# Cross attention: row sums from ScalarE's accumulator, taken off the row maxima as a logarithm

## The reference

```python
qp = q @ Wq.T
k, v = jnp.split(latent_kv @ Wkv_expand.T, 2, axis=-1)      # 16 heads of 32
scores = jnp.einsum('bhqd,bhkd->bhqk', qh, kh) / jnp.sqrt(32)
scores = jnp.where(causal, scores, finfo.min)               # 256 x 256 for each batch and head
attn = jax.nn.softmax(scores, axis=-1)
out = jnp.einsum('bhqk,bhkd->bhqd', attn, vh)
return out.reshape(b, sq, 512) @ Wout.T
```

## Time and profile before

| | |
|---|---|
| times of three runs | 1062.95 (median), 1061.24, 1067.86 us |
| profiled execution | 1065.82 us, span 1064.1 us |
| mean granted clock of PE over the span | 0.977 |
| busy: PE, DVE, ACT, POOL | 1005.4, 669.4, 454.0, 261.4 us |
| cross attention | from 293.9 us to 550.8 us of the span |

### The profile page before, as it was taken

How to read it: one execution, slowest core, us unless ns; L and a number is a source line. 1 busy time by engine, 2 the same in 40 slices (tenths; PEclk the granted TensorE clock), 3 DMA queues, 4 the chain that set the end, 5 groups by cost and what they waited for, 6 DMA issues and landing times. The chain is left out here.

```text
span 1064.1 us, 18069 instructions
## 1 busy us (share of the span) xinstructions
PE 1005.4 (94%) x6352; PEld 857.4 (81%) x6352; DVE 669.4 (63%) x1515; ACT 454.0 (43%) x803; POOL 261.4 (25%) x362
## 2 busy tenths in 40 slices
PE   7899999999979999999979989999999999999996
PEld 5688888888868888887757778989988999778785
DVE  4837546378266677776566837777777775253576
ACT  5523414236125455454534216666665664221210
POOL 4610010103143333333412012312231220503040
PEclk9999999999987999999998989999999999899999
DMA  4503013022786788877622247788778783615042
GB/s 162 194 1 119 0 59 148 0 79 97 210 224 148 218 204 233 232 218 200 212 104 73 82 144 251 246 268 279 236 263 276 253 258 110 221 36 178 19 158 79
DMA packets 87248, 172.79 MB, mean 162 GB/s; under 512 B 8113, under 2 KB 36017, under 8 KB 85393
## 3 DMA queue, kind: packets, MB, share of 16 engines
q1 hardware_dynamic: 81072, 150.21, 45.2%
q0 software_dynamic: 6112, 21.76, 6.2%
HBM read 131.05 MB, written 37.49 MB: 158 GB/s over the span
## 5 line engine op out<-in xcount | busy, mean ns | idle before, releaser
L45 PE MATMUL a_ps_proj<-region_a_rounded,arena 128*128 128x512 f32 x272 | 107.8, 396 | 10.7 <-DVE region_a_rounded L369 6.2
L45 PE MATMUL e_ps_h<-e_x_lo,e_gu_hi 128*128 128x256 f32 (+1 forms) x384 | 110.5, 288 | 3.8 <-DVE e_x_lo L2189 1.3
L962 DVE CUSTOM_DVE_ANT_0 b_dump<-b_ps_s,b_mask 128x128 f32<-128x128 f32 (+1 forms) x256 | 80.3, 353 | 48.5 <-PE b_ps_s L1157 45.3
L46 PE MATMUL e_ps_h<-e_x_hi,e_gu_lo 128*128 128x256 f32 (+1 forms) x384 | 107.5, 280 | 0.0
L47 PE MATMUL e_ps_h<-e_x_hi,e_gu_hi 128*128 128x256 f32 (+1 forms) x384 | 107.4, 280 | 0.0
L46 PE MATMUL a_ps_proj<-region_a_rounded,arena 128*128 128x512 f32 x272 | 106.7, 392 | 0.0
L47 PE MATMUL a_ps_proj<-region_a_rounded,arena 128*128 128x512 f32 x272 | 106.6, 392 | 0.0
L388 DVE SCALAR_TENSOR_TENSOR f_region_b<-a_ps_proj,a_taps,f_region_b 128x510 f32<-128x510 f32 (+2 forms) x96 | 71.7, 746 | 41.0 <-ACT f_region_b L328 38.7
L2195 DVE TENSOR_TENSOR e_gu_lo<-f_region_a,e_gu_hi 128x704 fp32r<-128x704 f32 x92 | 81.2, 886 | 16.6 <-ACT e_gu_hi L2101 16.1
L848 ACT ACTIVATE b_pt<-b_ps_x 128x384 f32<-128x384 f32 x128 | 61.8, 487 | 60.0 <-PE b_ps_x L1181 59.8
L762 POOL TENSOR_SCALAR_AFFINE_SELECT b_pt<-b_pt 128x256 f32<-128x256 f32 x128 | 54.3, 428 | 123.0 <-ACT b_pt L848 122.5
(11 more groups left out here) (418 smaller groups left out, 2665.5 us busy)
## 6 DMA issues: line engine op xcount, KB each, us to landing
f_region_a<-we_gate_up SPq DMA_DIRECT2D x88, 352.0 KB, 5.2
qk_split<-arena SPq DMA_DIRECT2D x24, 512.0 KB, 5.4
y_slots<-f_region_b SPq DMA_DIRECT2D x16, 512.0 KB, 3.7
f_x_next<-x SPq DMA_DIRECT2D x6, 1024.0 KB, 7.4
b_sk<-qk_split SPq DMA_DIRECT2D x24, 256.0 KB, 4.1
b_sq<-qk_split SPq DMA_DIRECT2D x24, 256.0 KB, 5.7
f_region_a<-we_down SPq DMA_DIRECT2D x12, 512.0 KB, 4.4
f_region_b<-we_down SPq DMA_DIRECT2D x11, 512.0 KB, 4.1
```

Of the source, the lines that this page charges most:

```text
L45: pe.matmul(out, a_hi, b_lo, start=first, stop=False)
L46: pe.matmul(out, a_lo, b_hi, start=False, stop=False)
L962: ins = dve.tensor_tensor_reduce(dump[:, n % 2, cols], ps_s[:, n % 2, cols], mask[:, cols], -1.0, 3e38, ALU.add, ALU.min, peak[:, u, k, i: ...
```

## The change

The sums of the exponentials are no longer made by PE. As before, DVE's maxima leave the masked scores, negated (now also multiplied by the scale of the scores), in `dump`; ACT now takes the exponential of each head's `dump`, with the row's maximum as bias, and its accumulator gives the row sum (`totals`, two instructions for each head, on 128 and 256 columns). When eight heads are done, ACT takes the logarithm (`logs`), DVE takes it off the negated maxima (`shifts`), and that, in place of the maxima, is transposed and loaded below the queries. The second exponentials are then normalised already. `pick`, `invert`, `keep`, `spread_out` and `normalize` go.

To make room on ACT, DVE rounds x, queries and values from PSUM by a copy, and also waits for that copy before it subtracts; ACT rounds `ps_o` straight into `a_hi`, DVE makes `a_lo`. The two DMAs of `load_peaks` move from SP to POOL. `peaks` stands in step 3 of both halves, `shifts` in step 1. DVE's maxima wait for the totals of two heads before (`dump` has two buffers).

```diff
@@ gpsimd
+            def load_peaks(b, u):
+                pool.wait_ge(m_lo_done, half_count(b, u))
+                for r, m in ((K_ROWS, m_hi), (K_ROWS + 1, m_lo)):
+                    pool.dma_start(sq[b % 2][r:r + 1, u].bitcast(F32), m[:, u].bitcast(F32)).then_inc(m_loaded, 16)
...
-                        if t and u == 0 and i in (3, 4):
-                            rest(t - 1, i - 3)
+                        if u == 0 and i == 4:
+                            load_peaks(t, 1)
+                        if u == 1 and i == 4 and real(t + 1):
+                            load_peaks(t + 1, 0)
@@ scalar
-            act.preload_act_table_set("exp_and_others")
+            act.preload_act_table_set("natural_log_exp_and_others")
...
+            def totals(b, u, i):
+                n = order(b, u, i)
+                act.wait_ge(max_done, n + 1)
+                for k, cols in ((0, slice(0, P)), (1, slice(P, 3 * P))):
+                    ins = act.activation(dump[:, n % 2, cols], dump[:, n % 2, cols], ACT.Exp, scale=-1.0,
+                                         bias=peak[:, u, k, i:i + 1], accum_out=total[:, u, k, i:i + 1])
+                ins.then_inc(total_done, 1)
+
+            def logs(b, u):
+                act.wait_ge(total_done, order(b, u, UH - 1) + 1)
+                if b:
+                    act.wait_ge(shift_done, half_count(b - 1, u))
+                act.activation(log_total[:, u], total[:, u], ACT.Ln).then_inc(log_done, 1)
...
                         exponent(t, u, i)
+                        if i == 0 and (u == 0 or real(t + 1)):
+                            totals(t + u, 1 - u, UH - 1)
+                            logs(t + u, 1 - u)
+                        if i and real(t + 1):
+                            totals(t + 1, u, i - 1)
                         fill(t, u, i)
...
-                keep(t)
-            for u in range(2):
-                attended(B - 1, u)
+                for u in range(2):
+                    attended(t, u)
@@ vector
             def turned(b, u):
-                dve.wait_ge(xkq_hi_done, x_count(b, u))
+                dve.wait_ge(xkq_ready, x_count(b, u))
...
+                dve.tensor_copy(hi, ps_pj[:, u]).then_inc(xq_hi_done, 1)
+                dve.wait_ge(xq_hi_done, x_hi_count(b, u))
+                dve.tensor_tensor(lo, ps_pj[:, u], hi.bitcast(F32), ALU.subtract).then_inc(xkq_lo_done, 1)
...
+            def shifts(b, u):
+                dve.wait_ge(log_done, half_count(b, u))
+                if b:
+                    dve.wait_ge(m_ready, half_count(b - 1, u))
+                dve.tensor_tensor(shift[:, u], peak[:, u], log_total[:, u], ALU.subtract).then_inc(shift_done, 1)
...
                 if n >= 2:
-                    dve.wait_ge(max_done, n - 1)
+                    dve.wait_ge(total_done, n - 1)
...
-                        if t >= 1 and u == 0 and i in (1, 2):
-                            normalize(t - 1, i - 1)
-                        if u == 0 and i == 5:
+                        if t >= 1 and u == 0 and i < 2:
+                            attended(t - 1, i)
+                        if u == 0 and i == 1:
+                            shifts(t, 1)
+                        if u == 0 and i == 4:
                             peaks(t, 1)
-                        if u == 1 and i == 2 and real(t + 1):
+                        if u == 1 and i == 1 and real(t + 1):
+                            shifts(t + 1, 0)
+                        if u == 1 and i == 4 and real(t + 1):
                             peaks(t + 1, 0)
@@ tensor
             def peaks(b, u):
-                pe.wait_ge(max_done, order(b, u, UH - 1) + 1)
+                pe.wait_ge(shift_done, half_count(b, u))
...
             def attend(b):
-                pe.wait_ge(exp_done, HEADS * (b + 1) - 1)
-                for c in range(DC):
-                    pe.wait_ge(cut_done, HEADS * b + HC * (c + 1))
-                    for r in range(BT):
-                        for h in range(HC):
-                            mm = pe.matmul(ps_x[h * HD:(h + 1) * HD, 0, r * P:S], pick[:, c],
-                                           pt[:, HC * c + h, 2 * r * P:(2 + r) * P],
-                                           start=c == 0 and r == 0, stop=c == DC - 1 and r == BT - 1)
-                mm.then_inc(sums_o_ready, 1)
...
-                        if t >= 1 and u == 0 and i == 1:
-                            spread_out(t - 1)
-                        if u == 0 and i == 4:
+                        if u == 0 and i == 3:
                             peaks(t, 1)
```

More of the change, by code:

```diff
@@ L551, in cross_attention @@
         peak = sb("peak", [P, 2, BT, UH])
+        total = sb("total", [P, 2, BT, UH])
+        log_total = sb("log_total", [P, 2, BT, UH])
+        shift = sb("shift", [P, 2, BT, UH])
         m_split = sb("m_split", [HD + UH, 2, S], F32R)
@@ L777, in _ @@
             pool.memset(bln.power[:], -0.5).then_inc(consts, 1)
[L778 to L785, removed]
+            pool.wait_ge(consts, 5)
             for k in sk:
                 pool.memset(k[K_ROWS:M_ROWS].bitcast(F32), 1.0).then_inc(consts, 1)
-            pool.wait_ge(consts, 14)
+            pool.wait_ge(consts, 7)
+            load_peaks(0, 0)
             for t in range(0, B):
@@ L866, in fill @@
                             keys(b, 1)
[L867 to L879, removed]
-                for u in range(2):
[L881 to L885, removed]
             def attended(b, u):
-                act.wait_ge(a_raw_done, 2 * b + u + 1)
+                act.wait_ge(o_ready, half_count(b, u))
                 if b:
                     act.wait_ge(out_ready, 2 * b)
-                cs = slice(UC * u, UC * u + UC)
-                act.activation(a_hi[:, cs], a_raw[:, cs], ACT.Copy).then_inc(a_hi_done, 1)
-            values(0, 0)
-            values(0, 1)
+                act.activation(a_hi[:, UC * u:UC * u + UC].rearrange("p c t -> p (c t)"), ps_o[:, u], ACT.Copy)\
+                    .then_inc(a_hi_done, 1)
+            first_values(0)
+            totals(0, 0, 0)
+            first_values(1)
+            totals(0, 0, 1)
             context(GB)
-            turned(GB, 0)
-            turned(GB, 1)
+            totals(0, 0, 2)
+            totals(0, 0, 3)
             keys(GB, 0)
-            queries(GB, 0)
+            for i in range(4, UH):
+                totals(0, 0, i)
+            logs(0, 0)
+            totals(0, 1, 0)
+            totals(0, 1, 1)
             peaks(0, 0)
             keys(GB, 1)
-            queries(GB, 1)
-            act.wait_ge(consts, 12)
-            act.activation(spread[:], spread_from.rearrange("p c h m -> p c (h m)"), ACT.Copy).then_inc(r_hi_o_kept, 1)
+            for i in range(2, UH - 1):
+                totals(0, 1, i)
             for t in range(B):
@@ L1026, in fill @@
                             norm_step(o, i - 3)
+                    if real(t + 1) and i in (5, 6):
+                        values(t + 1, i - 5)
             dve.wait_ge(consts, 3)
@@ L1039, in _ @@
                     queries(GB, 0)
-                if i == 1:
+                    shifts(0, 0)
+                if i == 2:
                     peaks(0, 0)
@@ L1062, in _ @@
                                                      ALU.mult).then_inc(ln_step, 1)
-                invert(t)
             for u in range(2):
-                normalize(B - 1, u)
-            for u in range(2):
-                dve.wait_ge(a_hi_done, 2 * (B - 1) + u + 1)
-                cs = slice(UC * u, UC * u + UC)
-                dve.tensor_tensor(a_lo[:, cs], a_raw[:, cs], a_hi[:, cs].bitcast(F32), ALU.subtract).then_inc(a_lo_done, 1)
+                attended(B - 1, u)
             shared.rest_part(dve, 2)
@@ L1172, in below_peak @@
                 if i == 0:
-                    pe.wait_ge(consts, 14)
-                    if b and u == 0:
-                        pe.wait_ge(rinv_lo_done, inverse_count(b - 1))
+                    pe.wait_ge(consts, 7)
                     pe.wait_ge(m_loaded, 32 * (2 * b + u + 1))
@@ L1209, in attend @@
                     if c % UC == UC - 1:
[L1210 to L1222 removed]
+                        mm.then_inc(o_ready, 1)
             def fill(t, u, i):
```

162 lines of the change are left out of this document (53 added, 109 removed).

## The result

The changed kernel takes 1072.54 us (median of 7 runs, 1068.77 to 1074.73), the kernel before 1063.89 (7 runs, 1059.04 to 1067.86): ratio 1.0076, 95% interval 1.0053 to 1.0100. It is slower by 0.5 to 1.0%, where I had forecast 4 us less.

What follows compares the result with a forecast made beforehand. The prediction took PE to bound batches 1 to 5. Its terms, +3.9 - 3.0 - 2.0 - 3.7 - 3.2 + 4, summed to -4.0 us, against the median of 1062.95 giving 1059 (1052 to 1068); the range with rivals was 1047 to 1076.

Steps and rivals of the forecast that it cites:

- step of ACT (pair of totals): ACT's work per head: two totals at 0.97 us (0.71 to 1.17), with the head's exponent 1.35.
- prologue and batch 0: Start of the cross attention: totals and DVE's added copies make it 3.9 us longer (-0.5 to +7.5).
- batches 2 to 5 at full clock: Middle batches: DVE's longer chain in the head gives back most of PE's gain, leaving -0.5 us each.
- clock: PE in the heads: waits bring half clock, some 1.6 us lost, in half of five heads: +4 us (0 to +8).
- batch 6: Batch without projections: ACT's queue and the closing loop take 24.1 us for 26.1, so -2.0 (-5 to +1).
- batch 7: Last batch: row sums, spread and a POOL wait go, -4.9, loads on POOL add 1.2: -3.7 us.
- tail: After the last attention products: reciprocal, spread, multiplication and rounding no longer delay the output, -3.2 us.
- ACT bounds the middle: Batches 1 to 5: accumulator reads don't overlap, a pair costs 1.37 us, ACT needs 32 per batch; about 1079, chance 0.15.
- the head is milder: Start of each batch: pair at 0.71 us, clock holds, DVE's copy overlaps better; 1047 to 1051 us, chance 0.25.
- The queue of POOL: Maxima's loads moved to POOL: taken at 3.3 us, covered in batches 1 to 5, about 1 showing in 0 and 7.
- The rival with late loads: POOL's loads land 6 us after issue: batches 0 and 7 +3 each, 1 to 5 +1.3; about 1069, chance 0.05.
- The third rival: Clock falls in every head, twice as long, and through batch 0's products: +16 and +2.7 us, about 1074, chance 0.15.

Runs made afterwards that it cites:

- e5: The changed kernel with 13 idle identity transpositions on PE ahead of its wait for the shifts in batches 1 to 5: 1067.20 us, ratio 1.0028.
- e7: The changed kernel without the accumulator in the totals, ones standing in for the sums: 1070.18 us, ratio 1.0052.
- e6: The changed kernel with the next stage's loads of x at the end of SP's list, behind the third weights part: 1065.11 us, ratio 1.0023.
- e2: The changed kernel with the two small loads of maxima issued by SP again, at their old places: 1069.82 us, ratio 1.0072.
- e12: e10 plus idle PE products in batch 6, maxima's loads on POOL, SP's finished-batch store and inputs behind stacks and keys' store: 1050.82 us, ratio 0.9880.
- e8: e6 with the head reordered, second queries' copy ahead of maxima, and attention's output rounded ahead of the third weights part: 1064.94 us, ratio 1.0000.
- e10: e8 with maxima's loads on SP, second half's first, batch 0's normalisations on DVE, output's first half added before third weights' rest: 1064.52 us.

## Why the prediction was wrong, step by step

| term | predicted | measured in the profile |
|---|---|---|
| step of ACT (pair of totals) | 1.35 (0.97) | 1.25 (0.87) |
| prologue and batch 0 | +3.9 | +5.3 (52.64 for 47.38) |
| batch 1 | -1.0 | +0.8 |
| batches 2 to 5 at full clock | -2.0 | -1.8 (119.3 in e5, for 121.1) |
| clock | +4 | +5.8 (125.1 less those 119.3) |
| batch 6 | -2.0 | -2.1 |
| batch 7 | -3.7 | +1.5 |
| tail | -3.2 | -1.7 |
| sum | -4.0 | +7.8 (7.7 from end to end) |

- **What was right.** That most of PE's gain of 3.6 us a batch is given back in the head: in batches 2 to 5 the shifts' wait is 1.77 and the query starts at T+6.9 (383.50, T being 376.6), both as worked out. The rivals in which ACT bounds the middle, and in which the head is milder, are out: at full clock the batches take what the forecast said. The price of the pair holds, too: without the accumulator (e7) a pair takes 0.69 us where the sum has 0.71, and a read adds 0.09 where it has 0.13.
- **What was luck.** Batch 6 came out as forecast, but its 24.1 was ACT's queue at a step of 1.35; at the measured 1.25 that sum is 22.5, and in e7, where a pair costs 0.18 less, the batch is only 0.4 shorter. PE's waits and its clock of 0.93, neither of them in that sum, are in the batch; what paces it was not settled.
- **The step that failed is "The queue of POOL".** It took 3.3 us for the rows' load from one row of the kernel before and let "about 1 us" show in batch 7. The load took 1 us of issue and 5.6 to land, PE stood for 4.05, and the clock of batch 7 fell to 0.92: 5.2 us of the 11.7 between forecast and profile. With the bulk moved (e6) batch 7 takes 16.4, the 3.7 less that were forecast. The rival with late loads had the length, about 6 us, at a chance of 0.05, but the wrong cause: POOL's path is not slow, it is the bulk in front of the rows (e2, e6), and by the timelines the removal of the row sums is what set it there. The same took 1.53 us in batch 1, where SP, no longer held by the rows, sends the inputs (0.6 MB) and the keys' store (0.5) ahead of them; without it batch 1 would stand at -0.7 (e2 has it there). The inputs alone are not the cause: in e12 they go later, and 1.9 us of wait stay; what else counts among the keys' store, the residuals (1 MB) and the stacks was not separated.
- **The clock** was sized at half of five heads; it fell in four of five, at 1.4 us per head, near the 1.6 of the earlier trace rows. The third rival had nearly the count; its price of twice as long was too high, so that its 1074 lies near the measured time by chance.
- **The tail** was to start "at once". ACT's rounding of the third part of the weights stands ahead of the attended there, and its load landed late, so PE waited 1.54. I had read the tail's terms for PE and DVE and not ACT's queue. With the order turned round in e8 that wait is gone, and with DVE's in e10 the next one shrank.
- **Prologue and batch 0**: the sum is off by 1.4. Its own terms as written add up to about 4.6 (25.3 - 18.8 - 0.97 - 2.62 + 1.7) and not to 3.9. The first exponent comes 4.2 later and not 1.7: PE's two longest waits before it, 2.18 and 2.88 us where they were 1.23 and 1.78, are for DVE, and I had let half of DVE's copies fall into its waits. How much of it comes from DVE's maxima waiting for the totals was not separated. Batch 0 itself is 1.0 longer for the 2.2 that 3.9 leaves it, with a step of 1.25 for 1.35.

## What to carry to other kernels

When work is taken off the critical engine, ask also what its end releases: here a last exponents' product lets 3.4 MB go, and the 2.6 us of row sums that stood behind it had helped to keep that bulk clear of a 16 KB load that PE waits for. A small urgent load needs its place in time against the bulk, not another queue. A wait of 1 to 2 us on PE can cost as much again in clock, and filling it with idle products shows in one run whether it does.

## What the runs showed of the hardware

- The accumulator of ACT is read by an instruction of its own, 190 ns on average (256 of them), which adds about 0.1 us from start to start.
- A load of 8 KB issued by POOL lands in 1.7 us on quiet DMA engines and in 5.2 to 5.6 with 2 to 2.6 MB moving beside it; from SP's queue PE's wait was as long.
- In e5 13 useless products in a wait of PE kept the granted clock at 1.00 where it had been 0.95, and made each of four batches 1.5 us shorter.
